# Moving an attention layer into the next layers' block, its units read and released bank by bank

## The reference, cut to what matters

```python
x = layernorm(x + L0_attn(x)); x = layernorm(x + L0_ffn(x))       # not touched
# L1_attn: 16 heads of 8; batch and sequence change places, 512 positions attend to each other
q, k, v = (x @ W.T for W in (Wq, Wk, Wv)); q, k = rope(q), rope(k)
x = layernorm(x + softmax(q @ k.T / sqrt(8)) @ v)
# L1_ffn, twice: heads of 64, windows of 64 keys that see the window before
h = shift_token(x); q, k, v = split(h @ wqkv)
q, k = rotary_xpos(l2norm(q) * qs, l2norm(k) * ks)
x = x + local_attention(q, k, v) @ wo
h = norm(shift_token(x)) @ w1 + b1; a, g = split(h); x = x + (a * gelu(g)) @ w2 + b2
# layernorm(x + all of this)
```

## Time and profile before

| | us |
|---|---|
| median of 3 runs (1691.41 to 1694.0) | 1692.29 |
| the profiled execution, whole | 1688.91 |
| its span in the trace | 1686.3 |
| attention1, from its first instruction to the barrier behind it | 865.1 to about 1159.4 |
| first and last exponentials of attention1 start | 887.8, 1143.5 |
| first row maximum of the local attention | 1177.0 |

### The profile page before, as it was taken

The page is one execution under the profiler, slowest core; times in us unless marked ns, Lnnn a source line. Parts: engine busy times, 40 slices in busy tenths (PEclk is TensorE's granted clock), DMA queues, the critical chain, the costliest instruction groups (busy, mean ns, idle before and its releaser), DMA issues. The chain is left out here.

```text
span 1686.3 us, 30347 instructions
## 1 busy us (share of the span) xinstructions
PE 1528.0 (91%) x10286; PEld 1043.9 (62%) x10286; DVE 1137.9 (67%) x2216; ACT 1072.2 (64%) x2347; POOL 519.4 (31%) x476
## 2 busy tenths in 40 slices
PE   7999999999889999999969888886899988899986
PEld 5777777777667888888824333332666655566654
DVE  2666666667567777777766777763777753777755
ACT  2555555555477888888826666652777754777751
POOL 1222222222232222111110000014676733676632
PEclk9999999999979999999967989986999999999998
DMA  7000000000012211222000000000000000000000
GB/s 232 2 2 0 0 0 0 0 0 0 2 53 76 76 65 60 75 75 71 29 1 0 1 1 1 1 1 1 1 2 1 1 1 0 2 1 1 1 2 25
DMA packets 18991, 36.34 MB, mean 22 GB/s; under 512 B 5764, under 2 KB 11008, under 8 KB 16704
## 3 DMA queue, kind: packets, MB, share of 16 engines
q1 hardware_dynamic: 18896, 35.09, 6.2%
HBM read 33.91 MB, written 1.18 MB: 21 GB/s over the span
## 5 line engine op out<-in xcount | busy, mean ns | idle before, releaser
L904 DVE TENSOR_TENSOR m_hidp<-m_hid,m_hidp 128x512 fp32r<-128x512 f32 x256 | 180.3, 731 | 76.1 <-ACT m_hidp L826 75.2
L305 ACT ACTIVATE a_prob<-ps,a_negmax 128x512 f32<-128x512 f32 (+3 forms) x256 | 134.0, 526 | 146.5 <-DVE a_negmax L381 146.5
L831 ACT ACTIVATE m_hid<-ps,pre_w 128x512 f32<-128x512 f32 x256 | 175.6, 687 | 61.6 <-PE ps L1040 58.3
L1366 DVE TENSOR_REDUCE c_sb_negmax<-ps 128x2 f32<-128x1024 f32 x128 | 155.9, 1222 | 63.0 <-PE ps L1503 62.8
L1095 PE MATMUL ps<-m_hidp,m_w2p 128*128 128x512 f32 x768 | 192.2, 399 | 0.0
L1040 PE MATMUL ps<-m_xp,m_w1p 128*128 128x512 f32 x768 | 189.2, 396 | 0.0
L1304 ACT ACTIVATE c_sb_pT<-ps 128x1024 f32<-128x1024 f32 x128 | 129.5, 1025 | 91.9 <-PE ps L1519 90.5
L265 POOL TENSOR_TENSOR a_qk_r<-a_qk_c,a_qk_s 128x512 f32<-128x512 f32 x64 | 81.4, 1273 | 325.8 <-DVE a_qk_s L372 325.8
L1848 ACT ACTIVATE l_sb_prob<-ps,l_sb_negmax,l_sb_rn 128x192 f32<-128x192 f32 (+1 forms) x256 | 124.1, 494 | 74.6 <-DVE l_sb_negmax L1947 74.6
L1040 PEld LDWEIGHTS ps<-m_xp,m_w1p 128*128 128x128 f32 x768 | 145.2, 190 | 36.3 <-issue 3.0
L1095 PEld LDWEIGHTS ps<-m_hidp,m_w2p 128*128 128x128 f32 x768 | 145.4, 189 | 35.2 <-issue 0.3
(11 more groups left out here) (232 smaller groups left out, 3229.0 us busy)
## 6 DMA issues: line engine op xcount, KB each, us to landing
m_gate_all<-m_gates_d SPq DMA_DIRECT2D x16, 1024.0 KB, 4.7
pre_w<-w1T SPq DMA_DIRECT2D x14, 258.0 KB, 2.7
pre_w<-w2T SPq DMA_DIRECT2D x14, 256.0 KB, 2.8
pre_wqkv<-wqkv SPq DMA_DIRECT2D x2, 768.0 KB
keep_x<-x SPq DMA_DIRECT2D x1, 1024.0 KB, 9.3
out<-keep_x SPq DMA_DIRECT2D x4, 256.0 KB, 2.3
keep_xT<-xT SPq DMA_DIRECT2D x1, 768.0 KB, 4.9
pre_m_w<-l_w SPq DMA_DIRECT2D x2, 341.0 KB
```

Source lines behind the costliest of these rows:

```text
L305: nc.scalar.activation(prob[:, u % 4, 0:width(p)], score_ps(b, p, j)[:, 0:width(p)], ACT.Exp, bias=negmax[:, u:u + 1], accum_out=den[:, b ...
L831: nc.scalar.activation(hid[:, c % 2, f, :], ps[:, f, :], ACT.Gelu, bias=w1[:, k, FF + f:FF + f + 1]).then_inc(gelu_done, 1)
L904: nc.vector.tensor_tensor(hidp[:, c % 2, 1, f, :], hid[:, c % 2, f, :], hidp[:, c % 2, 0, f, :], ALU.subtract).then_inc(low_done, 1)
L1366: nc.vector.tensor_reduce(negmax[:, m % 2, i, g:g + 2], ps[:, pair(max_turn(k)), :], AX.X, ALU.max, negate=True).then_inc(max_done, 1)
```

## The change

1. **One block.** `attention1` no longer opens a block. It returns its four engine programs, and `layers` calls them at the front of its own. The barrier goes, and the memsets and tables of the local attention now run ahead of attention1 (those of the MLP behind tile 0).
2. **Overlap.** Tile 0's head moves into the last quad: `project_qk(0, 0)` at r 3, its copies, ropes and squares between the unit work, the rest behind the last unit. Tile 0's step (`first`) takes in the end of the last batch (`moments`, `standard`, `turn_x`, halves). Batch 0's `turn_x` moves to the end of quad 14, and the ends of batches 0 to 2 are ordered anew on DVE.
3. **Overlaid buffers.** The tiles of the local attention and MLP become views of `pT` and `v_all`.
4. **Bank by bank.** Each unit's two banks are waited for, read and released singly: two `tensor_reduce` of 128x512 for one of 128x1024, two exponentials of 128x512 for one of 128x1024, and a semaphore increment on each finished bank. The last 8 turns go round over two pairs.
5. **Order in a quad.** ACT copies `lead` ahead of `copy_o`. DVE's `remain(m+3, 0)` stands one `maxima` earlier.
6. **Second layer.** In the first MLP's last batch, `project_v` of tiles 0 and 1 and `copy_v(1, 1)` move ahead of the third `up` and `gelu`.

```diff
+    def pair_no(turn):
+
+        return turn % 3 if turn < 2 * ALL - NUNIT else 1 + (turn + 1) % 2
...
+    def wait_bank(pe, turn, i):
+
+        last = turn - 1
+        while last >= 0 and pair_no(last) != pair_no(turn):
+            last -= 1
+        if last < 0:
             return
...
+            for i in range(2):
+                act.wait_ge(e_mm, 2 * e + i + 1)
+                nc.scalar.activation(pT[:, m % 2, g + i, t, :], ps[:, pair(exp_turn(e)).start + i, :], ACT.Exp,
+                                     scale=SCALE).then_inc(exp_done, 1)
...
-            nc.vector.tensor_reduce(negmax[:, m % 2, i, g:g + 2], ps[:, pair(max_turn(k)), :], AX.X, ALU.max,
-                                    negate=True).then_inc(max_done, 1)
+            for i in range(2):
+                dve.wait_ge(max_mm, 2 * k + i + 1)
+                nc.vector.tensor_reduce(negmax[:, m % 2, t, g + i:g + i + 1], ps[:, pair(max_turn(k)).start + i, :],
+                                        AX.X, ALU.max, negate=True).then_inc(max_done, 1)
...
+            if m + 3 < NQ:
+                leading(m + 3, 0)
+            if m == NQ - 1:
+                local.copy_qk(0)
             if m:
                 copy_o(m - 1)
-            if m + 3 < NQ:
-                leading(m + 3, 0)
             exps(e + 5)
+            if m == NQ - 1:
+                local.squares(0)
             exps(e + 6)
             if m + 1 < NQ:
...
+            for g in (g0, g0 + 1):
+                r = slice(32 * g, 32 * g + 32)
+                wait_bank(pe, u, g - g0)
...
+                if m == NQ - 2 and r == 7:
+                    turn_x(0)
+                if m == NQ - 1 and r == 3:
+                    local.project_qk(0, 0)
+                if m == NQ - 1 and r in (4, 5):
                     turn_x(r - 3)
                 if m == NQ - 1 and r > 5:
                     sums(m, r - 6)
+        local.project_v(0, 0)
+        local.project_v(1, 1)
         turn_o(NQ - 2)
         sums(NQ - 1, 2)
         sums(NQ - 1, 3)
+        local.project_qk(1, 1)
         turn_o(NQ - 1)
-        turn_x(LAST)
+        local.turn_qk(0, 0)
+        local.turn_qk(0, 1)
+
+        return turn_x
+
+
...
+        def first(moments, standard, high_half):
+            rowmax(0, 0, 0)
+            rowmax(0, 0, 1)
+            moments(NB - 1)
+            squares(1)
+            copy_pT(0, 0, 0)
+            standard(NB - 1)
+            rope_sum(1)
+            rowmax(0, 0, 2)
+            rowmax(0, 0, 3)
+            high_half(NB - 1)
+            copy_pT(0, 0, 2)
+            reciprocal(0, 0)
+            rope_c(2, 2)
...
+        def first(turn_x):
+            scores(0, 0, 0)
+            project_qk(2, 2)
+            turn_p(0, 0, 0)
+            turn_p(0, 0, 1)
+
+            scores(0, 0, 1)
+            values(0, 0, 0)
+            turn_qk(1, 0)
+            turn_p(0, 0, 2)
+            turn_x(NB - 1)
+            turn_qk(1, 1)
+            turn_p(0, 0, 3)
+            project_v(2, 2)
...
+            up(LAST, 0)
+            up(LAST, 1)
             local.project_v(0, 0)
+            local.project_v(1, 1)
+            up(LAST, 2)
...
+    att = attention1(nc, keep, tiles)
+    tiles.share()
...
-        run(attention1, io, keep)
```

More of the change, by code:

```diff
@@ L1638 @@
-Mlp = namedtuple("Mlp", "gpsimd scalar vector tensor x1_ev hn_ev hn_done gelu_done hid_done x2_ev f_norm_done")
+LocalScalar = namedtuple("LocalScalar", "step first last copy_qk squares copy_v copy_qT copy_kT")
+LocalVector = namedtuple("LocalVector", "clear step first last rope_c squares rope_sum")
+LocalTensor = namedtuple("LocalTensor", "step first last project_qk project_v turn_qk")
+Mlp = namedtuple("Mlp", "gpsimd scalar vector tensor first_banks batch_ready score_banks sum_bank f_norm_done")
@@ L1907, in last, with first @@
             mlp.copy_hn(0)
-        return LocalScalar(start, step, last, copy_qk, squares, copy_v, copy_qT, copy_kT)
+        def first(low_half):
+            exps(0, 0, 0)
+            exps(0, 0, 1)
+            copy_pT(0, 0, 1)
+            copy_qk(2)
+            exps(0, 0, 2)
+            exps(0, 0, 3)
+            copy_qT(1, 1)
+            low_half()
+            copy_pT(0, 0, 3)
+            copy_kT(1, 1)
+            squares(2)
+            copy_v(2, 2)
+        return LocalScalar(step, first, last, copy_qk, squares, copy_v, copy_qT, copy_kT)
     def vector(dve):
@@ L2010, in last @@
             add_y(n)
-        return LocalVector(clear, start, step, last, rope_c, squares, rope_sum)
+        def first(moments, standard, high_half):
[12 more added lines that the diff above has]
+            rope_c(2, 2)
+        return LocalVector(clear, step, first, last, rope_c, squares, rope_sum)
     def tensor(pe, ahead):
@@ L2174, in last @@
             output(n)
-        return LocalTensor(start, step, last, project_qk, project_v, turn_qk)
+        def first(turn_x):
[11 more added lines that the diff above has]
+            project_v(2, 2)
+        return LocalTensor(step, first, last, project_qk, project_v, turn_qk)
     return Local(tables, gpsimd, scalar, vector, tensor, qkT_ev, exp_done, pT_ev, o_ev, y_add)
@@ L2317, in last @@
             gelu(LAST, 1)
+            local.copy_v(1, 1)
             gelu(LAST, 2)
@@ L2324, in last @@
             local.squares(1)
-            local.copy_v(1, 1)
         return MlpScalar(shift, copy_hn, batch, last)
@@ L2545, in _ @@
         local[0].clear()
+        att.gpsimd(pool, local[0])
+        local[0].step(0)
         mlp[0].clear()
-        local[0].start()
-        for n in range(NT):
+        for n in range(1, NT):
             local[0].step(n)
@@ L2571, in _ @@
         local, mlp = [a.scalar(act) for a in locals_], [a.scalar(act) for a in mlps]
-        local[0].start()
-        for n in range(NT - 1):
+        local[0].first(att.scalar(act, local[0]))
+        for n in range(1, NT - 1):
             local[0].step(n)
@@ L2589, in _ @@
         locals_[0].tables(nc.vector)
-        local[0].start()
-        for n in range(NT - 1):
+        local[0].first(*att.vector(dve, local[0]))
+        for n in range(1, NT - 1):
             local[0].step(n)
```

224 lines of the change are left out of this document (119 added, 105 removed).

## The result

The changed kernel takes 1664.39 us, the median of four runs (1661.48 to 1666.25). Four runs of the kernel before beside it have a median of 1691.85 (1685.52 to 1694.0). The ratio is 0.9837, with a 95% interval of 0.9819 to 0.9855: 27.5 us less, about twice the 14.0 that were forecast, and 2.6 us under the range. The profiled execution took 1666.25 us against 1688.91, 22.7 us less; some 5 us of the medians' difference are in no trace. So the traces are compared from that mark on.

What follows compares the result with a forecast made beforehand. PE was taken to bound the loop of units, and a serial chain through the engines the stretch behind it. Gains of 3 (loop), 10.4 (overlap) and 0.6 (second layer) made 14.0 us: 1678.3 us, range 1667 to 1687.

Steps and rivals of the forecast that it cites:

- (a): Loop, steps 4 to 7: remain one maximum earlier makes st ready before PE's projection; the 0.99 us wait goes.
- (b): Loop, steps 4 to 7: lead ahead of copy_o makes the exponentials of step 5 start about 0.45 us later.
- (c): Loop, step 6: max_scores starts as before, ends half a us later on its second bank; 0.5 of 0.99 us is left.
- the term for the increments: Loop: twice as many increments and waits on PE cost 3.5 us, between bounds of nothing and 7.7.
- the clock stays up in the loop: Rival, chance 0.14: less idle lifts the loop's clock from 0.89 to 0.95, 12.8 us more gain, 1665.5 us.
- The last quad: Last quad: turn_x(0) delays step 0 by 2.2 us, PE idles 4.5 ahead of turn_x(2); step 6 comes 5.4 later.
- The tail and tile 0: After the last quad: first row maximum 12.4 us earlier, less 2 (1 to 4) at tile 0's step; gain 10.4.
- the prediction's own sign: Forecast wrong if tile 1's scores came over 3 us later behind the first row maximum than the earlier 9.85.
- their rival: Rival, chance 0.17: increments cost 6.4 us over 128 units, so the loop gains only 0.1; 1681.2 us.
- POOL's queue: Rival, chance 0.10: work queued on POOL ahead of norms(1) holds tile 1, costing 5.4 us for 2; 1681.7 us.
- ACT in steps 5 to 7: Rival, chance 0.07: ACT bounds these loop steps, each quad pays 1.4 against 0.99; loop loses 6.6 us, 1687.9 us.
- the slow rival: Rival, chance 0.06: new idle pattern holds the loop's clock at 0.82, losing 17.3 us; 1695.6 us.

Runs made afterwards that it cites:

- e6: The kernel before with an increment on each of a unit's two last matmuls, banks still waited for and read whole; 1695.27 us, ratio 1.0027.
- e5: The kernel before with only DVE's remain one maximum earlier, lead still behind copy_o; 1651.3 us, ratio 0.9767.
- e15: e5 with the scores of each quad's eighth unit of maxima made four times in place; 1669.82 us, ratio 0.9891.
- e11: The changed kernel with whole units, lead behind copy_o, and rope_c(0, 0) moved behind standard(2) and two halves on DVE; 1647.31 us, ratio 0.9738.
- e2: The kernel before with item 5 (order in a quad) alone; 1667.73 us, ratio 0.9855.
- e3: The kernel before with items 4 and 5 (banks and order), without the overlap; 1672.89 us, ratio 0.9892.
- e8: The changed kernel with item 4 undone except the round over two pairs in the last 8 turns; 1659.94 us, ratio 0.9822.
- e14: The changed kernel with rope_c(0, 0) behind standard(2) and turn_x(0) behind step 0 of the last quad; 1654.79 us, ratio 0.9804.

## Why the prediction missed

**The loop (forecast 3 us, measured 18.6).** The wait on `st` went, as in (a), and was worth 1.07 us a quad, not 0.99. (b) was right to the tenth: 0.40 to 0.42 for 0.45. (c) was right in its picture, with the second matmul of step 6 late by half a us. Together (b), (c) and the increments took 0.61 of the 1.07 (13.58 to 14.19), where (a) to (c) and the 3.5 us left 0.23 a quad. Over 15 quads the measured 0.46 is 6.9 us. The difference of 0.23 a quad is mostly the term for the increments, 3.5 us over 13 quads or 0.27 and measured at 0.09 (e6), and the wait's 0.08. The larger part, 18.6 - 6.9 = 11.7 us, is the clock: three long quads for six, and shorter ones. The step that failed is the sum of the loop, which took its granted clock as fixed: from 890 to 1080 it went from 0.89 to 0.97. The rival "the clock stays up in the loop" had the rising clock and 12.8 us for it, for a time of 1665.5; it was given 0.14. That its time is within 1.2 us of the measured one is partly luck: it had 15.8 us for the loop, 2.8 too few, and 10.4 for the tail, 7.5 too many, and the medians lie 5 us further apart than the traces. The range was said to hold most of this rival, but 1665.5 lies below its end of 1667. What was held against it, "about 1.5 of 2 us idle per quad stay", doesn't decide: e5 keeps 1.16 us of idle per quad and has no long quad at all. The rival's reason, that less idle time lifts the clock, isn't shown as the cause either (e15).

**The last quad (5.4 us given away; measured 12.6).** Step 6 stood 17.2 us behind the mark before and stands 29.8 behind it now. turn_x(0) made step 0 late by 2.65 us (forecast 2.2). From step 0 to project_qk it took 13.2 us (forecast 9.0), project_qk itself 3.52 for 1.98, and from its end to step 6 it took 8.3 (7.3), with a gap ahead of turn_x(2) of 5.36 (4.5), released by DVE's standard as forecast. So 5.8 of the 7.2 us that the forecast lacks lie in steps 0 to 3 and project_qk. It is the same error: the forecast took these durations from the trace before, where they ran partly or wholly at full clock, and now the granted clock was 0.50 from 1106.5 to 1122. The sign "steps 0 to 3 should stay at 1.65 us" was no reading of the kernel before: there step 1 stood 2.21 us behind step 0 and step 2 2.67 behind step 1.

**The tail and tile 0 (gain 10.4; measured 2.9).** From the last unit's scores to the first row maximum it was 16.2 us (1135.71 to 1151.87) where 17 were forecast, so this part held. Tile 1's scores came 13.4 us behind the row maximum, 3.1 more than before for 2 forecast and within its bounds of 1 to 4. By the prediction's own sign (over 3 us more than 9.85, counted to the mask's matmul ahead of the scores) it is just past the edge: 12.9, 3.05 more. Of the shortfall of 7.5 us, 7.2 are the last quad's; at tile 1 1.1 were lost and behind the last unit's scores 0.8 won. e11 shows that the overlap can give its forecast size, a tail of 52.9 for 62.7 in e5, once nothing holds standard(2).

How much the overlap gives depends on the clock of the kernel that it is set against. Before, the steps of the last quad ran at either clock, and the tails without overlap go from 62.7 to 69.7 us. With the overlap in its old form steps 0 to 2 ran at half clock in every run. Against e2 it gave 9.1 us, against e3 6.2, against the kernel before 2.8, and against e5 1.0.

**The second layer (0.6; measured none).** The table load came 22.2 us earlier, 1411.27 for 1433.50, only 0.2 more than tile 1's scores, and at the end 21.8 are left.

**The other rivals.** Increments cost 4.6 us; the interval, 1 to 8, still holds the 6.4 of their rival, while 16 full quads at 0.09 would be 1.4. On top of item 5 the banks with them cost, not gave: e3 is 5 us above e2, the changed kernel 4.5 above e8, though with overlapping intervals. ACT in steps 5 to 7 did carry the order's price, but the other half of item 5 paid it more than twice. POOL's queue did hold tile 1, though less than its rival had it: the turn of k waited 0.90 us for POOL's `norms` (the row at 1161.76). That k_n ended 9.7 us behind the row maximum, 3.5 later than before, when PE took it up 1.4 us after it was made. With this slack gone some 2.2 us are POOL's, and the other 0.9 is project_v at half clock behind it (1.92 for 1.02). The loop's clock rose where the slow rival had it fall.

## What to carry to other kernels

Look at the granted clock of each stretch before pricing an edit. In this loop, which PE bounds and where the clock was below full, 1.07 us saved per round were worth twice that in the loop (31.8 us for 16), and 0.40 us added cost twice that in the whole time (13 us for 6), so the sum is wanted at both levels. Read, engine by engine, what stands behind each instruction that waits: one line moved ahead of a maximum gave 40 us here and one moved ahead of a rope 6.5, and an edit that looked like the first one's twin cost 13. Test the parts of a change alone, since here a good and a bad one arrived together.

## What was not expected of the hardware

The granted clock of a loop that repeats itself answers to less than half a us per round: 13.58 us a quad had it at 0.98 from 890 to 1080, 14.19 at 0.97 with three long quads, 14.65 at 0.89, 15.05 at 0.86. Long quads come with the length of the round even when the added time is work (e15). And in the changed kernel PE stayed at half clock for some 17 us without a gap, from turn_x(0) at 1106.57 into project_qk, which ended at 1124.35: mostly row-tiled matmuls of 32 rows and sums of 32 columns, busy 13.43 of 13.5 us from 1106.5 to 1120 at 0.50. The clock rose there inside project_qk, but in e8 and e14 it rose ahead of it, by step 3.
